# A 512-column product ahead of each score step of the row maxima, and doubled replications in the first six rounds of the scans

## The chip, the cores and the metric

The kernel runs on one core of one Trainium2 chip. The metric is the device time of one execution in microseconds (us). "PE" is TensorE (its weight loads are the separate engine name PEld), "DVE" is VectorE, "ACT" is ScalarE, "POOL" is GpSimd and "SP" is SyncE, which issues the transfers. The clock of PE that the profile calls granted has two levels here, 2.4 GHz (shown as 1.0) and 1.2 GHz (shown as 0.5); a value in between is the mean over a stretch that saw both.

## The reference

Eight images of 64 channels and 32 x 32 = 1024 tokens go through three layers:

```python
x = _mamba(...)            # W_in, causal conv, selective scan over 1024 tokens, gate, W_out
x = silu(group_norm(x)) + x_hsi
t = t + attention(layernorm(t))      # 8 heads of 8 channels, causal over 1024 tokens
t = t + moe(layernorm(t))            # 8 experts of 64 x 64, top 2 of 8 by a softmax router
```

The selective scan has 128 channels with 16 states each, h = exp(dt A) h + dt B x, y = C h.

## The kernel before

A program on every engine runs `pipeline`: twelve iterations, in each of which up to five images are in work at different stages: `a` (load), `c` (convolution, dt, B and C, then the scans), `p` (output of the scan layer, group norm, layer norm, queries and keys), `b` (attention) and `f` (projection and experts). Image `b` appears from the fourth iteration to the eleventh; `c` from the second to the ninth. So eight iterations hold attention work, and in the last two of these there is no `c`. Below, such an iteration goes by the number of the image in its attention, 1 to 8; the clock of "image 5" is that of the fifth iteration with attention.

Each iteration has two phases.

**Row maxima (score phase).** Before the softmax the kernel needs the maximum of each row of scores. 48 score steps (`SCORE_STEPS`, line 334) go over row blocks i = 0 to 7 of 128 queries, in two quads of four heads. Step s computes on PE the scores of one block of 128 queries: for i below 4 two heads with 128(i+1) keys each, for i from 4 on one head with 512 + 128(i-3) keys; a product with a mask (128 columns, line 1202) is added on the diagonal. It writes the bank pair 4, 5 or 6, 7 by turns (line 1194), and DVE then takes the maxima of the pair with one TENSOR_REDUCE (`row_maxima`, line 926). PE waits before step s until DVE is done with step s-2 (line 1192). Between the steps both engines carry the work of images `c` and `p`, at places written out by hand in the two tables `beside`: on PE, convolution at steps 1 and 2, the last folds at 1 to 3, gate projection at 5 and 6, output projection at 9 and 10, the product for dt at 11 and 12, the B product at 17 and 18, the C product at 20 and 21, the value projection at 24, transposes at 26, 33 and 34, the query and key projection at 37 and 38. These are float32 products, of which one of 512 columns is two instructions. PE executes all in program order, so a score step stands behind the work that was put before it.

**Scans and attention (round phase).** 28 rounds (`UNITS_IN`, line 336). A round holds up to two units of the scans for image `c`: `unit` (line 1253) replicates a half (512 columns) of the rows of dt and then of u over 128 partitions with a bf16 product each (`replicate`, line 1236), into the next bank of a ring of five (`free_bank`, which waits until the reader of five users earlier is done). ACT makes `decay` from the dt bank (line 762), DVE makes `drive` from the u bank (line 979), and DVE runs one scan (line 970) per two units; POOL multiplies by C (line 660); PE folds (line 1126). From the fifth round on a round also holds a step of the attention for image `b` (`weigh`, line 1302, exponentials on ACT at line 801, `add_values`, line 1317), and turns of image `f` (lines 1111, 1117, 1286). The first six rounds are four without an attention step, where `s` is `None`, and the steps s = 0 and 1; they hold 2, 2, 2, 1, 0 and 2 units.

The score phase ends with four small DVE operations on the maxima (lines 944 to 951) and eight transposes (`turn_maxima`, line 1229); SP takes the maxima out and into `q_stack` (lines 561 and 564) before the first attention step. SP issues all transfers in one order: the rows of dt and u in three parts (line 539), then the token-major copy, the parts of queries and keys, the maxima.

Of the kernel before, what the change touches and what calls it, by code (L numbers as in the profile page):

```python
# [12 lines left out]
BANK = 512  # L13
# [30 lines left out]
def mamba_attention_moe(nc, x, W_in, conv_w, conv_b, W_x, W_dt, b_dt, A_log, D, W_out, gn_gamma, gn_beta,  # L44
# [8 lines left out]
    DH = C // H  # L53
# [24 lines left out]
    with ExitStack() as ctx:  # L78
        def sb(name, shape, dt=F32):
            return ctx.enter_context(nc.sbuf_tensor(name, shape, dt))  # L80

        ps = ctx.enter_context(nc.psum_tensor("ps", [P, 8, BANK], F32))

        def banks(n, k=1):
            return ps[:, n:n + k, :].rearrange("p a b -> p (a b)")
# [39 lines left out]
        dt_rows = sb("dt_rows", [96, NG, T], BF16)  # L125
        u_rows = sb("u_rows", [96, NG, T], BF16)
# [11 lines left out]
        dt, u = read[:, 0, :], read[:, 1, :]  # L138
# [19 lines left out]
        q_stack = sb("q_stack", [P, H, T], BF16)  # L158
        k_stack = sb("k_stack", [P, H, T], BF16)
# [157 lines left out]
        def signal(name, per, base=0):  # L317
            return Signal(ctx, nc, name, per, base)
# [48 lines left out]
        dt_rep = signal("dt_rep", UNITS)  # L367
        u_rep = signal("u_rep", UNITS)
# [83 lines left out]
        def chunk(k):  # L452

            g, q = k % NG, k // NG
            return g, q, JG * g + q

        def halves(n):
            return slice(n * BANK, (n + 1) * BANK)

        def tokens(i):  # L460
            return slice(i * P, (i + 1) * P)
# [37 lines left out]
        def bank_read(user, c, b, f):  # L499

            kind, n = user
            return {"dt": (decayed, c), "u": (driven, c), "scores": (exped, b), "heads": (attn_ready, b),
                    "attn_t": (attn_t_copied, f), "proj": (t2_ready, f), "xn_t": (xnt_copied[1], f),
                    "router": (gate_centred, f), "expert": (weighted, f), "out_t": (x_out_copied, f)}[kind] + (n + 1,)
# [7 lines left out]
        with nc.Block() as block:  # L512
# [588 lines left out]
            def _(pe):  # L1101
                def program(_, c, p, b, f):

                    def project(weights, src, bank, h, rows=P):

                        return pe.matmul(ps[0:rows, bank + h, :], weights, src[:, halves(h)], start=True, stop=True)  # L1106

                    def to_channels(src, blocks, dst):

                        for n, i in enumerate(blocks):  # L1110
                            last = pe.transpose(dst[0:C, tokens(n)], src[:, i, :], ident[:, :])  # L1111
                        return last
# [75 lines left out]
                    def score_step(s):  # L1188

                        i, h0, nh = SCORE_STEPS[s]  # L1190
                        if s >= 2:
                            pe.wait_ge(row_maxed.sem, row_maxed.at(b, s - 1))
                        for hh in range(nh):
                            for h in range(i // QB + 1):
                                bank = 4 + 2 * (s % 2) + hh + h
                                diagonal = h == i // QB
                                w = P * (i % QB + 1) if diagonal else BANK
                                last = pe.matmul(ps[:, bank, 0:w], q_stack[0:9 * DH, h0 + hh, tokens(i)],  # L1198
                                                 k_stack[0:9 * DH, h0 + hh, h * BANK:h * BANK + w],
                                                 start=True, stop=not diagonal)  # L1200
                                if diagonal:
                                    last = pe.matmul(ps[:, bank, w - P:w], ident_bf[:, :], mask_q[:, :],  # L1202
                                                     start=False, stop=True)
                        last.then_inc(scores_ps.sem, 1)
# [21 lines left out]
                    def turn_maxima():  # L1226
                        pe.wait_ge(max_parts_ready.sem, max_parts_ready.at(b, 1))
                        for i in range(TB):
                            last = pe.transpose(banks(ACC).bitcast(BF16)[0:3 * H, tokens(i)],
                                                max_parts[:, i, :, :].rearrange("p r h -> p (r h)"), ident_bf[:, :])  # L1230
                        last.then_inc(max_t_ps.sem, 1)

                    def replicate(k2, bank, rows):

                        g, q, _ = chunk(k2 // 2)
                        return pe.matmul(bank, pick[:, q, :, :].rearrange("p n e -> p (n e)"),  # L1236
                                         rows[:, g, halves(k2 % 2)], start=True, stop=True)
# [4 lines left out]
                    def free_bank(user):  # L1242

                        place = places[user]
                        bank = RING[place % len(RING)]
                        if place >= len(RING):
                            read_by, batch, count = bank_read(users[place - len(RING)], c, b, f)
                            pe.wait_ge(read_by.sem, read_by.at(batch, count))
                        elif b and bank > ACC:
                            pe.wait_ge(row_maxed.sem, row_maxed.at(b, NSCORE))  # L1250
                        return banks(bank)

                    def unit(k2):
                        if k2 == 0:
                            pe.wait_ge(dt_rows_in.sem, dt_rows_in.at(c, 16 * 3 * NG))
                            pe.wait_ge(c_copied.sem, c_copied.at(c, 1))
                        replicate(k2, free_bank(("dt", k2)), dt_rows).then_inc(dt_rep.sem, 1)
                        if k2 == 0:
                            pe.wait_ge(u_rows_in.sem, u_rows_in.at(c, 16 * 3 * NG))
                        replicate(k2, free_bank(("u", k2)), u_rows).then_inc(u_rep.sem, 1)  # L1260

                    def take_turn(turn):

# [30 lines left out]
                    def weigh(s, heads):  # L1294

                        n, quad, half, j = KEY_STEPS[s]
                        lo = max(half * BANK, j * P)
                        w = (half + 1) * BANK - lo
                        diagonal = lo == j * P
                        for hq in heads:  # L1300
                            head, bank = quad * QUAD + hq, free_bank(("scores", QUAD * s + hq))
                            last = pe.matmul(bank[:, 0:w], k_stack[0:KQ, head, tokens(j)],  # L1302
                                             q_stack[0:KQ, head, lo:lo + w], start=True, stop=not diagonal)
                            if diagonal:
                                last = pe.matmul(bank[:, 0:P], ident_bf[:, :], mask_k[:, :],  # L1305
                                                 start=False, stop=True)
                            last.then_inc(weights_ps.sem, 1)
# [25 lines left out]
                    for n, (s, units, turns) in enumerate(ROUNDS):  # L1333
                        at_step = b and s is not None
                        if at_step:
                            if s == 0:
                                pe.wait_ge(max_in.sem, max_in.at(b, 16))
                            weigh(s, range(QUAD - 1))
                        if c and units:
                            unit(units[0])  # L1340
                        if b and n == 0:
                            turn_maxima()
                        if at_step:
                            if s > 0:
                                add_values(s - 1)
                            weigh(s, (QUAD - 1,))
                            if s - LAG in LAST_STEP:
                                heads_to_tokens(LAST_STEP.index(s - LAG))
                        if c:
                            for q, h, at in FOLDS:  # L1350
                                if at == n:
                                    if q == 0 and h == 0 and p:
                                        pe.wait_ge(qk_rest.sem, qk_rest.at(p, 1))
                                    fold_round(c, q, h)
                            for k2 in units[1:]:
                                unit(k2)
                        if f:
                            for turn in turns:
                                take_turn(turn)
# [8 lines left out]
                    for read_by, (batch, count) in last_read.items():  # L1368
                        pe.wait_ge(read_by.sem, read_by.at(batch, count))
                pipeline(pe, program)  # L1370


# [20 lines left out]
```

## Time and profile before

| | us |
|---|---|
| median of 3 runs | 1633.64 |
| lowest and highest | 1631.91, 1634.67 |
| the profiled execution, whole | 1626.1 |
| its span, first to last instruction | 1624.0 |
| mean granted clock of PE over the span | 0.761 |
| busy: PE, DVE, ACT, POOL | 1260.7, 1171.9, 704.3, 512.2 |

The profiled execution is 7.5 us below the median of the runs. PE's busy time counts a pipelined matmul from its start to its modelled end, so two matmuls in a row overlap; the distance between their starts is what one costs.

### The profile page before, as it was taken

The numbers are of one execution on the slowest core, as the hardware profiler recorded it, in microseconds if no ns is written. First come the engines' busy times: TensorE is split into PE (matmuls) and PEld (weight loads), VectorE is DVE, ScalarE is ACT, GpSimd is POOL, SyncE is SP. The second block draws the span as 40 slices with busy tenths as digits, with TensorE's granted clock in tenths as the row PEclk, the third lists the DMA queues.
The fourth block names the chain that finished last, engine by engine and source line by source line (L and its number), as shares of the span: only waits on it lengthen the run. The fifth ranks groups of instructions, "written<-read, shape, count | busy, mean of one in ns | idle before, by whom it ended". The sixth has DMA issues, their size and how long they took to land. (4 is left out here: it accounts for less than half of the span.)

```text
span 1624.0 us, 17597 instructions
## 1 busy us (share of the span) xinstructions
PE 1260.7 (78%) x6388; PEld 499.9 (31%) x6388; DVE 1171.9 (72%) x1388; ACT 704.3 (43%) x1298; POOL 512.2 (32%) x272
## 2 busy tenths in 40 slices
PE   2455346888888987888887987888888988899894
PEld 1111111323233333333333323333233324433433
DVE  3396398787678968887679867887688867348345
ACT  1423322347434762376335642476326631460470
POOL 2454454344334332342243333342144321000000
PEclk9567556659966998589867997599758985695696
DMA  1100320021202111201211120201220120020000
GB/s 38 45 1 13 83 53 13 7 68 30 55 8 68 30 32 38 67 1 30 62 29 45 30 50 19 68 10 23 47 61 14 30 49 17 19 51 21 3 14 7
DMA packets 25863, 54.87 MB, mean 34 GB/s; under 512 B 8531, under 2 KB 8919, under 8 KB 23448
## 3 DMA queue, kind: packets, MB, share of 16 engines
q1 hardware_dynamic: 25776, 53.73, 14.6%
q8 instruction: 51, 0.84, 0.2%
q14 instruction: 36, 0.29, 0.1%
HBM read 28.15 MB, written 12.98 MB: 25 GB/s over the span
## 5 line engine op out<-in xcount | busy, mean ns | idle before, releaser
L926 DVE TENSOR_REDUCE row_max<-ps 128x1 f32<-128x768 f32 (+7 forms) x384 | 355.9, 952 | 142.2 <-PE ps L1202 139.6
L660 POOL TENSOR_TENSOR read<-state,c_rep 128x1024 f32<-128x1024 f32 x128 | 303.9, 2374 | 466.2 <-DVE state L970 450.6
L801 ACT ACTIVATE probs<-ps 128x512 f32<-128x512 f32 (+3 forms) x768 | 329.5, 496 | 144.7 <-PE ps L1305 86.5
L970 DVE TENSOR_TENSOR_SCAN state<-decay,drive 128x1024 f32<-128x1024 f32 x128 | 357.1, 2790 | 1.8 <-POOL read L660 1.1
L1198 PE MATMUL ps<-k_stack,q_stack 72*128 72x512 bf16 (+3 forms) x768 | 280.6, 456 | 83.2 <-DVE row_max L926 64.3
L1302 PE MATMUL ps<-q_stack,k_stack 75*128 75x512 bf16 (+3 forms) x768 | 222.8, 353 | 32.7 <-DVE drive L979 17.8
L979 DVE TENSOR_TENSOR drive<-ps,b_rep 128x512 f32<-128x512 f32 x256 | 169.6, 676 | 105.7 <-PE ps L1236 105.0
L762 ACT ACTIVATE decay<-ps,a_scale 128x512 f32<-128x512 f32 x256 | 175.3, 696 | 116.8 <-DVE state L970 100.1
L1236 PE MATMUL ps<-dt_rows,pick 96*128 96x512 bf16 x256 | 120.5, 471 | 96.9 <-DVE drive L979 69.5
L1317 PE MATMUL ps<-probs,v_aug 128*32 128x512 f32 (+3 forms) x1536 | 177.4, 536 | 4.1 <-ACT acc_sb L790 1.6
L1198 PEld LDWEIGHTS ps<-k_stack,q_stack 72*128 72x128 bf16 x768 | 73.8, 116 | 274.2 <-DVE row_max L926 171.4
L1302 PEld LDWEIGHTS ps<-q_stack,k_stack 75*128 75x128 bf16 x768 | 76.2, 102 | 245.4 <-ACT probs L801 89.4
L1202 PE MATMUL ps<-mask_q,ident_bf 128*128 128x128 bf16 x512 | 137.7, 278 | 0.0
L1236 PE MATMUL ps<-u_rows,pick 96*128 96x512 bf16 x256 | 120.8, 472 | 19.9 <-DVE attn L996 5.5
L1305 PE MATMUL ps<-mask_k,ident_bf 128*128 128x128 bf16 x512 | 110.4, 235 | 0.0
L597 POOL TENSOR_TENSOR ln_s<-ln_s,minus_half 128x8 f32<-128x8 f32 x16 | 26.3, 1643 | 262.2 <-DVE ln_s L904 262.2
L1202 PEld LDWEIGHTS ps<-mask_q,ident_bf 128*128 128x128 bf16 x512 | 65.2, 127 | 62.2 <-issue 54.2
L1236 PEld LDWEIGHTS ps<-dt_rows,pick 96*128 96x128 bf16 x256 | 27.4, 107 | 161.3 <-DVE drive L979 104.2
L1061 DVE TENSOR_TENSOR moe<-ps,gate_e 128x512 f32<-128x512 f32 x64 | 43.8, 685 | 44.9 <-PE ps L1286 44.9
L1126 PE MATMUL ps<-read,fold 128*32 128x512 f32 x512 | 74.6, 683 | 0.8 <-POOL read L660 0.8
L1106 PE MATMUL ps<-xc,w_bc 128*128 128x512 f32 x64 | 57.8, 1015 | 22.4 <-ACT b_rep L719 18.2
L1286 PE MATMUL ps<-w_expert,xn_t 96*128 96x512 f32 x128 | 69.3, 653 | 0.8 <-ACT decay L762 0.8
(169 smaller groups left out, 1281.6 us busy)
## 6 DMA issues: line engine op xcount, KB each, us to landing
q_stack<-q_parts_dram SPq DMA_DIRECT2D x48, 192.0 KB
k_stack<-k_parts_dram SPq DMA_DIRECT2D x48, 192.0 KB
dt_rows<-read SPq DMA_DIRECT2D x96, 64.0 KB, 2.0
u_rows<-read SPq DMA_DIRECT2D x96, 64.0 KB, 2.0
k_parts_dram<-read SPq DMA_DIRECT2D x40, 128.0 KB, 2.4
q_parts_dram<-read SPq DMA_DIRECT2D x24, 128.0 KB, 2.3
xs<-in_x SPq DMA_DIRECT2D x8, 256.0 KB, 3.5
residual<-in_x SPq DMA_DIRECT2D x8, 256.0 KB, 9.6
```

Of the source, the lines that this page charges most:

```text
L660: pool.tensor_tensor(read[:, k % (2 * NG), :], state[:, k % 2, :], c_rep[:, :], ALU.mult)\
L762: act.activation(decay[:, k % 2, halves(h)], bank_of(("dt", k2)), ACT.Exp, scale=a_scale[:, j:j + 1])\
L801: act.activation(probs[:, e % (2 * QUAD), 0:w], bank_of(("scores", e))[:, 0:w], ACT.Exp, scale=SCALE).then_inc(exped.sem, 1)
L926: dve.tensor_reduce(row_max[:, i, h0:h0 + nh], scores[:, :, 0:P * (i + 1)], AX.X, ALU.max, negate=True).then_inc(row_maxed.sem, 1)
L970: dve.tensor_tensor_scan(state[:, k % 2, :], decay[:, k % 2, :], drive[:, k % 3, :], 0.0, ALU.mult, ALU.add).then_inc(scanned.sem, 1)
L979: dve.tensor_tensor(drive[:, k % 3, halves(h)], bank_of(("u", k2)), b_rep[:, halves(h)], ALU.mult)\
L1198: last = pe.matmul(ps[:, bank, 0:w], q_stack[0:9 * DH, h0 + hh, tokens(i)], k_stack[0:9 * DH, h0 + hh, h * BANK:h * BANK + w], start=True, ...
L1202: last = pe.matmul(ps[:, bank, w - P:w], ident_bf[:, :], mask_q[:, :], start=False, stop=True)
L1236: return pe.matmul(bank, pick[:, q, :, :].rearrange("p n e -> p (n e)"), rows[:, g, halves(k2 % 2)], start=True, stop=True)
L1302: last = pe.matmul(bank[:, 0:w], k_stack[0:KQ, head, tokens(j)], q_stack[0:KQ, head, lo:lo + w], start=True, stop=not diagonal)
L1305: last = pe.matmul(bank[:, 0:P], ident_bf[:, :], mask_k[:, :], start=False, stop=True)
L1317: last = pe.matmul(ps[GW * hq:GW * (hq + 1), ACC, lo:BANK], v_aug[:, j, quad * QUAD + hq, :], probs[:, (QUAD * s + hq) % (2 * QUAD), 0:BAN ...
```

## The change

Each of the 48 score steps of an image first issues one more product of 72 rows, 128 weight columns and 512 moving columns, from the same stacks, into the first bank of the pair that the step is about to write. The step's own first product overwrites it. In the first six rounds of a round phase each unit issues the replication of dt twice and that of u twice into the same bank; only the second signals the reader. The waits are the same and stand where they stood.

```diff
+                    def keep_clock(bank, weights, src):
+
+                        pe.matmul(bank, weights, src, start=True, stop=True)
+
...
                         i, h0, nh = SCORE_STEPS[s]
                         if s >= 2:
                             pe.wait_ge(row_maxed.sem, row_maxed.at(b, s - 1))
+                        keep_clock(ps[:, 4 + 2 * (s % 2), :], q_stack[0:9 * DH, h0, tokens(i)],
+                                   k_stack[0:9 * DH, h0, 0:BANK])
...
-                    def unit(k2):
+                    def unit(k2, again=False):
                         if k2 == 0:
                             pe.wait_ge(dt_rows_in.sem, dt_rows_in.at(c, 16 * 3 * NG))
                             pe.wait_ge(c_copied.sem, c_copied.at(c, 1))
-                        replicate(k2, free_bank(("dt", k2)), dt_rows).then_inc(dt_rep.sem, 1)
+                        bank = free_bank(("dt", k2))
+                        if again:
+                            replicate(k2, bank, dt_rows)
+                        replicate(k2, bank, dt_rows).then_inc(dt_rep.sem, 1)
                         if k2 == 0:
                             pe.wait_ge(u_rows_in.sem, u_rows_in.at(c, 16 * 3 * NG))
-                        replicate(k2, free_bank(("u", k2)), u_rows).then_inc(u_rep.sem, 1)
+                        bank = free_bank(("u", k2))
+                        if again:
+                            replicate(k2, bank, u_rows)
+                        replicate(k2, bank, u_rows).then_inc(u_rep.sem, 1)
...
                         if c and units:
-                            unit(units[0])
+                            unit(units[0], s is None or s < 2)
...
                             for k2 in units[1:]:
-                                unit(k2)
+                                unit(k2, s is None or s < 2)
```

## Rows read from the trace of the kernel before

**Rows 1.** The page: busy time of DVE, granted PE clock in 40 slices, maxima group.

```profile
PE 1260.7 (78%) x6388; PEld 499.9 (31%) x6388; DVE 1171.9 (72%) x1388; ACT 704.3 (43%) x1298; POOL 512.2 (32%) x272
PEclk9567556659966998589867997599758985695696
L926 DVE TENSOR_REDUCE row_max<-ps 128x1 f32<-128x768 f32 (+7 forms) x384 | 355.9, 952 | 142.2 <-PE ps L1202 139.6
```

**Rows 2.** Busy time by stretch, score phases of images 2, 4, 5, 7 and 8.

```profile
core 0: us, PE busy (x) PEld busy (x) DVE busy (x) ACT busy (x) POOL busy (x), PEclk, DMA share, GB/s
428.40:502.10 73.70, 60.15 (x253) 24.56 (x252) 55.63 (x69) 21.50 (x22) 24.20 (x13) 0.73 0.21 47
...
780.80:858.40 77.60, 65.39 (x252) 25.88 (x251) 56.11 (x69) 21.54 (x22) 24.18 (x13) 0.67 0.23 53
960.30:1035.60 75.30, 62.30 (x252) 24.69 (x251) 55.87 (x70) 21.60 (x22) 24.21 (x13) 0.70 0.23 56
...
1318.70:1388.40 69.70, 58.32 (x230) 23.40 (x225) 52.78 (x68) 6.46 (x7) 11.09 (x7) 0.57 0.19 41
1459.60:1511.00 51.40, 45.35 (x172) 18.05 (x169) 44.78 (x49) 0.00 (x0) 0.00 (x0) 0.53 0.10 24
```

**Rows 3.** Busy time by stretch, columns as in rows 2: round phases, image 5 and 7.

```profile
1035.60:1045.10 9.50, 7.86 (x37) 4.56 (x38) 7.91 (x12) 5.76 (x9) 2.24 (x1) 0.64 0.37 85
1045.10:1056.00 10.90, 7.73 (x33) 2.68 (x32) 9.57 (x11) 4.87 (x10) 4.26 (x4) 0.53 0.01 2
1056.00:1139.20 83.20, 73.04 (x483) 27.89 (x480) 67.87 (x80) 55.58 (x122) 32.14 (x14) 0.96 0.10 21
1388.40:1407.50 19.10, 15.98 (x78) 9.04 (x78) 5.30 (x12) 6.59 (x16) 1.64 (x1) 0.50 0.02 6
```

**Rows 4.** Timeline of PE: 512-column products in a row, from 1034.08 and from 1056.52.

```profile
1034.08 0.63 PE L1236 MATMUL ps<-dt_rows,pick 96*128 96x512 bf16 x1
1034.51 0.63 PE L1236 MATMUL ps<-u_rows,pick 96*128 96x512 bf16 x1
...
1056.52 0.38 PE L1236 MATMUL ps<-dt_rows,pick 96*128 96x512 bf16 x1
1056.74 0.38 PE L1236 MATMUL ps<-u_rows,pick 96*128 96x512 bf16 x1
```

**Rows 5.** Timeline of DVE, steps 37 and 38: image 5, then image 2.

```profile
1020.54 0.96 DVE L926 TENSOR_REDUCE row_max<-ps 128x1 f32<-128x768 f32 x1 [1.60 <-PE ps L1202]
1023.10 1.82 DVE L926 TENSOR_REDUCE row_max<-ps 128x1 f32<-128x768 f32 x2 [1.60 <-PE ps L1202]
...
488.76 0.96 DVE L926 TENSOR_REDUCE row_max<-ps 128x1 f32<-128x768 f32 x1 [0.34 <-PE ps L1202]
490.06 2.82 DVE L926 TENSOR_REDUCE row_max<-ps 128x1 f32<-128x768 f32 x3 [0.34 <-PE ps L1202]
```

**Rows 6.** Line 926, waits for PE (us, times), image 4, window 795 to 804 us.

```profile
  PE ps L1202: 3.9, 3
```

**Rows 7.** Line 926, waits for PE (us, times), image 5, windows 976:984, 986:1003, 1003.5:1017.5, 1017.5:1035.7.

```profile
  PE ps L1202: 0.4, 1
...
  PE ps L1202: 6.3, 5
...
  PE ps L1202: 1.8, 5
...
  PE ps L1202: 3.8, 4
```

**Rows 8.** Timeline of ACT, image 5, after the last operation of the group norm on DVE.

```profile
988.69 1.20 ACT L683 ACTIVATE read<-ps,gn_v 64x1024 f32<-64x1024 f32 x1 [4.72 <-DVE gn_v L874]
...
993.26 0.99 ACT L719 COPY b_rep<-ps 128x1024 f32<-128x1024 f32 x1
```

**Rows 9.** Line 926, waits for PE (us, times), image 8, window 1459 to 1511 us.

```profile
  PE ps L1202: 6.2, 12
```

**Rows 10.** Timeline, image 8: maxima of 1024 columns, PE's two products and mask for one.

```profile
1478.80 4.82 DVE L926 TENSOR_REDUCE row_max<-ps 128x1 f32<-128x1024 f32 x4 [0.23 <-PE ps L1202]
1480.08 1.03 PE L1198 MATMUL ps<-k_stack,q_stack 72*128 72x512 bf16 x2 [0.31 <-DVE row_max L926]
```

**Rows 11.** Who waited for whom on DVE, image 5, window 1036 to 1058 us.

```profile
DVE drive L979 <- PE ps L1236: 3.8, 3, 1.7
```

## Prediction

> **What bounds the kernel now.** No engine is full: DVE works 72% of the span and PE's 78% counts overlapping matmuls whole, and PE's clock moves between its levels all the time [rows 1]. I read first the groups of instructions, for who is waited for: before the 384 maxima DVE stands idle 142.2 us, 139.6 of them for PE [rows 1]. Then the stretches by phase: a score phase takes 73.7 to 77.6 us for six images, 69.7 and 51.4 for the last two, with DVE busy 56, 52.8 and 44.8, at a mean clock of 0.73 down to 0.53 [rows 2]. The round phase runs at 0.96 once it is past its first 20 us, which are at 0.64 and 0.53 in image 5, and at 0.50 where there are no scans [rows 3]. So the low clock sits where the change adds products, and DVE waits for PE in just these stretches. In the score phase DVE is the path, with PE on it wherever a score step stands behind other work.
>
> Is the low clock what makes DVE wait? The same two steps tell it. At steps 37 and 38, behind the query and key projection, DVE idles 1.60 us each in image 5, and 0.34 each in image 2, where the clock was high for a few microseconds [rows 5]. At steps 9 to 11 image 4 loses 3.9 us at the low clock and image 5 loses 0.4 at the high one [rows 6, 7].
>
> **What is added, and its price.** 384 products in the score phases (48 x 8). In the rounds 9 units x 2 products x 8 images = 144. From start to start a 512-column product takes 0.43 us at the low clock and 0.22 at the high one [rows 4]. That is 528 products and 116 us of PE at the high clock, 227 at the low. What counts is whether PE with it is later than DVE. A steady pair of steps shows the margin. PE begins step s when DVE is done with s-2, and has the length of one reduction. At 1024 columns, low clock, the own work is 512 + 512 + 128 columns, 0.96 us at 0.43 per 512, and DVE still idles 0.23 per two steps; four reductions take 4.82 us [rows 10]. A pair there lasts 1.23 + 1.23; so handing over costs 1.23 - 0.96 = 0.27. At the high clock with the product the step has 1664 columns, 0.70 us, and 0.97 with the handing over: below the 1.14 of a reduction back to back, so hidden. At 640 columns it is 0.54 + 0.27 = 0.81 against about 0.74, a little exposed, less than now (0.64 + 0.27 = 0.91). So at the high clock a step with the product costs PE less time than the bare step at the low one for every block from i = 1 on (1280 columns against 768, 0.54 against 0.64 us), and the same at i = 0.
>
> **The sum, if the clock stays high through most of the score phase:**
> - Steps 36 to 47: 3.8 us idle now [rows 7]; 0.34 + 0.34 as in image 2 [rows 5] and 0.22 for each of two added products, 1.1. Saved 2.7 in six images (1 and 3 to 7), and +0.4 in image 2: -15.8.
> - Steps 9 to 11: 3.9 to 0.4 + 0.4, 3.1 saved in the four images that are low there (1, 4, 6, 7); +0.4 in the three that are high: -11.2.
> - Steps 16 to 21: 6.3 us idle [rows 7]. Not all is PE's. Behind the group norm ACT works without a pause from 988.69 to 994.25 (988.69 to 993.26 and 0.99 more) before the C product can start [rows 8]; that chain of 5.6 us stays. I take 1.3 saved in six images, for the B and C products at the high clock: -7.8.
> - Steps 24 to 35: 1.8 [rows 7] to 0.6, and somewhat more in image 7: -8.4 over seven images.
> - Image 8: 6.2 idle [rows 9] to about 3 (the value projection halves; blocks of 640 and 256 columns stay a little exposed): -3.
> - Steps 0 to 2, where the clock is high already and DVE waits for POOL, fold and score in a row: three products of 0.22 on the path in seven images: +4.6.
>
> Together -41.6. Waits of chains will still pull the clock down here and there; I take 85% of it: -35. Bounds: -50 (all of it and the steady pairs too) and, with the clock never up, the slower rival below.
> - First rounds with scans, images 1 to 6: DVE idles 3.8 us for replications [rows 11], at low clock. A doubled replication at the high clock costs what the single one costs now (2 x 0.22 against 0.43), so the units gain nothing; what gains is the other PE work there (transposes, weigh, values). At the high clock I get about 2 us an image back; if the clock falls in round 3 or 4, where PE has little, the two units of round 5 cost 4 x 0.43 = 1.7 more. I take -1 each, -6, with bounds -15 and +12.
> - The two iterations with scans but no attention: DVE is never late for PE there once running; only the first unit is exposed, up to 0.9 us each: +2.
> - First rounds of images 7 and 8, 19 us at 0.50 each [rows 3]: no product is added; if the phase is entered at the high clock, -2 each: -4.
>
> Sum -43: the profiled 1626.1 to 1583, and the median 1633.6 to about **1590**. (The profiled execution lies 7.5 below the median; I apply the same difference to both.)
>
> **What is late next.** Behind the score phase stand the rows of u. PE takes u's first replication at 1034.51 without waiting [rows 4], so the slack of the transfers isn't visible as a wait; if the tail of the score phase shrinks by 5 us and the chain from the layer norm through ACT, POOL and SP only by 3, the rest is lost before the first drive.
>
> A rule that speaks against the change: by the Trainium skill, "TensorE: Matmul & The Clock Gate", section "Part 3: Packing small matmuls — row/col tiling", a weight load overlaps running matmuls only when it goes to other row groups. The added product brings a load of 128 columns on the same rows. Rows 4 have a load for each product and 0.43 and 0.22 us from start to start, as long as the same product's columns at two clocks in the ratio of two, so I count no load. By the rule the result would be the fifth rival's.
>
> **The rivals.**
> 1. The clock rises for about half of the score phase only. Then half of the savings come (-20) and in the low half PE sets the pace with 0.43 per step wherever it is within 0.1 us of DVE: 192 steps, half of them, some 0.1 to 0.2 each, +14; first rounds +3. About 1631 to 1610, say 1620. For it: the clock falls now wherever chains of small operations stop PE (steps 13 to 17), and those stay. Chance 0.15.
> 2. The rows of u, or SP's issue order, become late, 2 to 3 us an image in six images: 1590 + 15 = 1605. Chance 0.10. It would show as DVE or PE waiting for a transfer at the head of the rounds.
> 3. Slower: the clock stays low in the score phases. In image 8 PE is already busy 45.4 of 51.4 us and yet at 0.53 [rows 2], so a busy PE alone doesn't raise it. Then each step is PE's: with 1664 columns 1.40 us against 1.23 now, with 1280 1.08 against 0.87, small ones +0.25; on average 0.19 x 384 = 73 us, and the first rounds 6 x 3 = 18: about 1725. It decides from the point where the added columns don't lift the clock. Against it: the added product makes up half again of the array's work in a step (512 on an average of 939 columns), and a PE that never waits is what stands ahead of the rises seen. A milder form (high in the middle, low around) ends at 1640 to 1660. Chance 0.09, both.
> 4. The doubled replications cost more than the score phases bring in beside them: low clock in round 5 and exposed doubling, +3 an image for six: 1590 + 24 = 1614. Chance 0.03.
> 5. The weight load isn't hidden: 0.10 us (24.7 us of 251 loads, [rows 2]) on each of the steps where PE is close, about half of 384, +19: 1609. The forecast's mechanism with a smaller gain; chance 0.03.
>
> **How the numbers follow.** Forecast 0.60, its own range 1572 to 1608. A measurement of this kernel can tell some 0.2%, 3.3 us. Faster by more: forecast 0.60, nearly all of rivals 1, 2, 4 and 5 and the forecast's neighbours, 0.85 together. Slower: rival 3 and a little of 1, 0.10. The same: 0.05. The range reaches down to all of the sum with the first rounds at their good bound (1633.6 - 50 - 15) and up into rival 1: 1568 to 1620.
>
> **What would show it.** Right: granted clock over 0.85 in the score phases of images 1 to 7; steps 37 and 38 idle about 0.55 each in every image; idle before line 926 from 142 us down to some 100; image 8's score phase near 48 us, image 4's near 68. The first rounds: mean clock over 0.75 and idle before line 979 below 3 us. Wrong: score phases at 0.6 with PE never waiting for DVE (rival 3), waits for transfers at line 1236 (rival 2), or a steady pair at 1024 columns that takes longer than 2.46 us.

## The result, and the profile after

| | before | after |
|---|---|---|
| median of 3 runs, us | 1633.64 | 1683.32 |
| lowest and highest | 1631.91, 1634.67 | 1674.09, 1683.7 |
| ratio, 95% interval | | 1.029 [1.025, 1.034] |
| profiled execution, its span | 1626.1, 1624.0 | 1674.1, 1672.0 |
| mean granted clock over the span | 0.761 | 0.809 |

The change makes the kernel 3% slower; 1590 was forecast. The clock did rise, and the time rose with it.

The same stretches as in [rows 2] and [rows 3], in the profile after (score phases of images 2, 4, 5, 7 and 8 and the sum over all eight, then image 5's round phase in three parts and the first rounds of image 7):

```profile
core 0: us, PE busy (x) PEld busy (x) DVE busy (x) ACT busy (x) POOL busy (x), PEclk, DMA share, GB/s
...
438.70:520.40 81.70, 72.44 (x301) 30.12 (x300) 56.17 (x69) 21.12 (x22) 23.88 (x13) 0.75 0.23 53
...
810.20:886.90 76.70, 67.04 (x301) 28.73 (x300) 56.05 (x69) 21.08 (x22) 24.02 (x13) 0.81 0.23 53
992.60:1070.40 77.80, 68.28 (x301) 28.99 (x300) 56.16 (x69) 21.14 (x22) 24.02 (x13) 0.80 0.23 56
...
1359.20:1429.30 70.10, 62.73 (x277) 28.00 (x270) 53.20 (x67) 6.46 (x7) 10.84 (x7) 0.70 0.19 40
1500.70:1561.00 60.30, 56.99 (x219) 25.09 (x217) 46.01 (x50) 0.00 (x0) 0.00 (x0) 0.58 0.09 20
sum 605.20, PE 536.58 PEld 230.06 DVE 435.99 ACT 133.06 POOL 156.25; mean PE 67.07 PEld 28.76 DVE 54.50 ACT 16.63 POOL 19.53
...
1070.40:1080.00 9.60, 8.33 (x37) 3.84 (x36) 6.71 (x12) 5.44 (x8) 0.94 (x1) 0.69 0.28 67
1080.00:1091.50 11.50, 8.10 (x41) 4.13 (x39) 10.19 (x11) 5.41 (x11) 4.86 (x3) 0.79 0.00 1
1091.50:1175.10 83.60, 73.77 (x491) 27.99 (x491) 68.20 (x81) 55.78 (x123) 33.05 (x15) 0.97 0.10 22
1429.30:1448.00 18.70, 15.51 (x74) 8.60 (x75) 5.34 (x13) 6.22 (x14) 1.64 (x1) 0.50 0.03 6
```

The sum of the score phases goes from 575.5 (the same eight stretches before) to 605.2 us: +29.7. The round phases go from 782.1 to 796.0, +13.9, and the first score phase starts at 270.8 instead of 266.4, +4.4. Together these are the 48.0 us between the spans. The mean clock of the score phases rises only from 0.66 to 0.75. Image 8 is the plainest: no other work stands between its steps but the value projection, PE is now busy 57 of 60 us, and the clock is 0.58. Before, that phase took 51.4. The 0.58 is the mean of two stretches: 9.2 us of a high clock that was there when the phase began, and the low one from then to the end, though PE is busy 49.55 of these 51.1 us.

```profile
1500.70:1509.90 9.20, 7.43 (x49) 3.59 (x48) 8.20 (x11) 0.00 (x0) 0.00 (x0) 1.00 0.57 130
1509.90:1561.00 51.10, 49.55 (x172) 21.50 (x170) 37.80 (x40) 0.00 (x0) 0.00 (x0) 0.50 0.00 0
```

Its last steps, by the timeline of DVE and of PE:

```profile
1555.47 1.22 DVE L926 TENSOR_REDUCE row_max<-ps 128x1 f32<-128x1024 f32 x1 [0.38 <-PE ps L1208]
1556.85 1.22 DVE L926 TENSOR_REDUCE row_max<-ps 128x1 f32<-128x1024 f32 x1 [0.16 <-PE ps L1208]
1558.35 1.22 DVE L926 TENSOR_REDUCE row_max<-ps 128x1 f32<-128x1024 f32 x1 [0.28 <-PE ps L1208]
1559.74 1.23 DVE L926 TENSOR_REDUCE row_max<-ps 128x1 f32<-128x1024 f32 x1 [0.16 <-PE ps L1208]
```

```profile
1555.22 0.63 PE L1110 MATMUL ps<-k_stack,q_stack 72*128 72x512 bf16 x1
1555.65 1.06 PE L1204 MATMUL ps<-k_stack,q_stack 72*128 72x512 bf16 x2
1556.50 0.31 PE L1208 MATMUL ps<-mask_q,ident_bf 128*128 128x128 bf16 x1
1556.75 0.61 PE L1110 MATMUL ps<-k_stack,q_stack 72*128 72x512 bf16 x1
```

The added product (line 1110) takes 0.43 us of the array (1555.22 to 1555.65), and none of these reductions begins without a wait: (1559.74 - 1555.47) / 3 = 1.42 us a step, where it was 1.23. PE issues product after product and the clock stays at 1.2 GHz.

Where the clock is high amid the other work, the steps behave as forecast. Steps 37 and 38 of image 4 (high clock) and of image 5 (low), answering to [rows 5]:

```profile
871.88 0.96 DVE L926 TENSOR_REDUCE row_max<-ps 128x1 f32<-128x768 f32 x1 [0.56 <-PE ps L1208]
873.40 2.97 DVE L926 TENSOR_REDUCE row_max<-ps 128x1 f32<-128x768 f32 x3 [0.56 <-PE ps L1208]
...
1053.23 0.96 DVE L926 TENSOR_REDUCE row_max<-ps 128x1 f32<-128x768 f32 x1 [2.03 <-PE ps L1208]
1056.21 0.96 DVE L926 TENSOR_REDUCE row_max<-ps 128x1 f32<-128x768 f32 x1 [2.03 <-PE ps L1208]
```

0.56 where 0.34 + 0.22 was worked out, and 2.03 = 1.60 + 0.43 where the clock is low.

The first drives of image 5's round phase, answering to [rows 11]; line 1242 is the replication:

```profile
1074.30 0.69 DVE L979 TENSOR_TENSOR drive<-ps,b_rep 128x512 f32<-128x512 f32 x1 [2.34 <-PE ps L1242]
...
1076.01 0.69 DVE L979 TENSOR_TENSOR drive<-ps,b_rep 128x512 f32<-128x512 f32 x1 [0.43 <-PE ps L1242]
...
1091.78 0.69 DVE L979 TENSOR_TENSOR drive<-ps,b_rep 128x512 f32<-128x512 f32 x1 [1.45 <-PE ps L1242]
```

Together with the drive after them they wait 6.6 us, where 3.8 were waited before: 2.34 was 1.49, 0.43 was nothing, 1.45 was 0.60. Each is later by one or two products at the low clock.

### The profile page after: what moved, and what is told of

Same layout as the page of the kernel before. It is cut to its first block and busy times, and to the rows that moved or that the text cites. A ratio compares the mean times of both kernels' runs of the same rounds, so it can differ in the third digit from the quotient of the medians.

```text
span 1672.0 us, 18653 instructions
## 1 busy us (share of the span) xinstructions
PE 1337.7 (80%) x6916; PEld 546.8 (33%) x6916; DVE 1173.2 (70%) x1388; ACT 704.5 (42%) x1298; POOL 511.8 (31%) x272
## 5 line engine op out<-in xcount | busy, mean ns | idle before, releaser
L1204 PE MATMUL ps<-k_stack,q_stack 72*128 72x512 bf16 (+3 forms) x768 | 262.8, 421 | 0.0
L1314 PE MATMUL ps<-q_stack,k_stack 75*128 75x512 bf16 (+3 forms) x768 | 219.0, 347 | 35.5 <-DVE drive L979 18.0
L1110 PE MATMUL ps<-k_stack,q_stack 72*128 72x512 bf16 x384 | 188.8, 492 | 61.2 <-DVE row_max L926 45.7
L1242 PE MATMUL ps<-dt_rows,pick 96*128 96x512 bf16 x328 | 138.1, 461 | 92.4 <-DVE drive L979 65.5
L1242 PE MATMUL ps<-u_rows,pick 96*128 96x512 bf16 x328 | 136.9, 457 | 19.7 <-DVE attn L996 6.9
L1208 PE MATMUL ps<-mask_q,ident_bf 128*128 128x128 bf16 x512 | 127.9, 258 | 0.0
L1204 PEld LDWEIGHTS ps<-k_stack,q_stack 72*128 72x128 bf16 x768 | 90.7, 118 | 87.2 <-issue 67.5
L1110 PEld LDWEIGHTS ps<-k_stack,q_stack 72*128 72x128 bf16 x384 | 42.6, 111 | 175.8 <-DVE row_max L926 119.1
L1208 PEld LDWEIGHTS ps<-mask_q,ident_bf 128*128 128x128 bf16 x512 | 61.0, 119 | 72.7 <-issue 47.6
L1242 PEld LDWEIGHTS ps<-dt_rows,pick 96*128 96x128 bf16 x328 | 33.2, 109 | 157.6 <-DVE drive L979 96.0
```

Source lines behind the costliest of these rows:

```text
L1110: pe.matmul(bank, weights, src, start=True, stop=True)
```

## The experiments

The theory after the result: PE's clock is not lifted in this kernel by products that use 72 of the array's 128 rows, though they keep PE busy; at the low clock the added product is then a plain cost. The rivals: that the doubled replications make the loss; that the other operands or the data matter and not the rows; that only the time PE is occupied counts. All runs have the kernel before beside them on the same chip. All times are medians in us, with the ratio to the kernel before and its interval.

**The two parts alone.** The argument `s is None or s < 2` taken out of the calls of `unit`, so that nothing is doubled (e1), and the call of `keep_clock` taken out (e2).

> The added 72-row product in the score steps alone, the replications as before. My theory after the result: the product costs 0.43 us wherever PE sets the pace, because the clock is not raised by products of 72 rows, although PE then never waits. It expects most of the loss here: the eight score phases some 30 us longer together (605 against 575 us in the two profiles), the round phases as before, so 1655 to 1670 us, and image 8's score phase near 60 us at a clock of about 0.58. The rival, that the doubled replications make the loss, expects 1630 to 1645.

1666.5, ratio 1.022 [1.017, 1.027]. Score phases 617.6 us in its profile, image 8's 63.5:

```profile
1496.80:1560.30 63.50, 61.79 (x219) 27.16 (x217) 46.35 (x49) 0.00 (x0) 0.00 (x0) 0.50 0.08 18
```

PE is busy 61.8 of 63.5 us and the clock is at 1.2 GHz throughout. The added score product by itself makes two thirds of the loss (34.7 of 51.7 us over the kernel before, with f1 below for the whole change).

> The doubled replications of the first six rounds alone. My theory: 10 to 18 us of the loss, from the round phases (796 against 782 us in the two profiles) and the start, so 1643 to 1652 us, idle before the drive (line 979) up by some 20 us. The rival, that the doubling is harmless and the loss is all in the score phase, expects 1631 to 1637.

1631.9 against 1631.8, ratio 1.001 [0.998, 1.004]. The time followed the rival, though the waits followed the theory: the page's group of the drive has

```profile
L979 DVE TENSOR_TENSOR drive<-ps,b_rep 128x512 f32<-128x512 f32 x256 | 169.9, 678 | 127.0 <-PE ps L1240 126.5
```

where the kernel before waits 105.7 us. This is taken up again below.

**The rows of the added product.** The doubling stays out; the product in the score step becomes

```diff
-keep_clock(ps[:, 4 + 2 * (s % 2), :], q_stack[0:9 * DH, h0, tokens(i)],
-           k_stack[0:9 * DH, h0, 0:BANK])
+keep_clock(ps[:, 4 + 2 * (s % 2), :], ident_bf[:, :],
+           mask_q[:, :].unsqueeze(1).to_broadcast([P, BANK // P, P]))
```

> As e1, but the added product has 128 rows (the identity as weights, the mask repeated four times as the moving operand), 512 columns as before. If the clock follows how many rows of the array the products use, it rises in the score phases: image 8's score phase at 0.85 or more and 47 to 50 us long, the time below that of e1 by 25 us or more and perhaps below 1625. If only the time that PE is occupied counts, or if the data count (these are mostly zeros), the result is that of e1, within 5 us, with image 8's score phase at 0.58 and 60 us.

1610.7, ratio 0.989 [0.985, 0.993]: 56 us below the same product with 72 rows. Score phases of images 3 and 8, and the sum of the eight:

```profile
609.00:679.80 70.80, 57.92 (x299) 25.54 (x298) 55.51 (x69) 21.84 (x22) 24.04 (x13) 0.95 0.23 54
...
1451.30:1498.10 46.80, 37.90 (x219) 17.16 (x217) 44.05 (x49) 0.00 (x0) 0.00 (x0) 1.00 0.12 27
sum 561.10, PE 463.83 PEld 201.82 DVE 431.45 ACT 136.15 POOL 156.28; mean PE 57.98 PEld 25.23 DVE 53.93 ACT 17.02 POOL 19.53
```

Image 8 runs at 2.4 GHz from its first step to its last. Its instructions are those of e1 but for the added product of each step (48 of the 219), which has 56 more rows and other operands. In this phase the forecast's step from the clock to the time holds: 46.8 us, where about 48 was forecast. Over all eight phases it doesn't; that is taken up under the reasons. On DVE, the reductions of 896 and 1024 columns stand back to back, the added product hidden as worked out:

```profile
1489.42 8.70 DVE L926 TENSOR_REDUCE row_max<-ps 128x1 f32<-128x896 f32 x8
```

The operands were changed too, so a control has the same identity and mask, cut to 72 rows (`ident_bf[0:9 * DH, :]` and `mask_q[0:9 * DH, :]`).

> The control for the 128-row product: the same operands (identity and repeated mask), cut to 72 rows, 512 columns, no doubling. If it is the rows that raise the clock, this is as slow as the product from the stacks, 1655 to 1675 us, image 8's score phase at a clock below 0.7 and over 57 us. If it was the other operands (other weights than the next product's, mostly zeros), it is as fast as with 128 rows, 1605 to 1620.

1664.6, ratio 1.023 [1.019, 1.027], image 8:

```profile
1493.40:1553.50 60.10, 56.87 (x219) 25.00 (x217) 45.99 (x49) 0.00 (x0) 0.00 (x0) 0.58 0.09 21
```

As slow as e1 with its other operands, and 54 us slower than e3, from which only the rows differ. Operands and data are out; the rows are left. Between the two, 96 rows:

> The added product of identity and repeated mask with 96 rows, between the 72 (1665 us) and the 128 (1611 us). 72 rows reach into the third group of 32 rows, 96 fill it. If the whole groups of 32 that a product touches count, it is as slow as 72 rows, 1655 to 1670; if the rows count one by one, it lies between, 1625 to 1650, with image 8's score phase partly at the high clock.

1632.9, ratio 1.001 [0.997, 1.005]. It lies between (1665, 1633, 1611), which speaks against whole groups of 32: 72 and 96 rows touch the same three. Images 6 and 8:

```profile
1145.00:1217.60 72.60, 60.97 (x299) 26.54 (x298) 55.84 (x69) 21.50 (x22) 24.00 (x13) 0.89 0.23 52
1462.50:1522.90 60.40, 57.17 (x219) 25.13 (x217) 45.95 (x49) 0.00 (x0) 0.00 (x0) 0.57 0.09 20
```

Where float32 products of the other images stand between the steps, 96 rows bring the phase to 0.89 (image 6 is at 0.78 in the profile of the change); where the steps stand alone they don't lift it, and image 8 is as slow as with 72. I had expected image 8 to be partly high; only its first 8.9 us are, as with 72 rows.

And 128 rows with fewer columns, `ps[:, bank, 0:288]` from `mask_q[:, 0:96]` repeated three times:

> The added product with 128 rows but only 288 columns, so that rows times columns are those of 72 rows and 512 columns. If the clock follows rows times columns, it falls short of the 512-column form: some of the score phases at the low clock, but the product is also shorter by 0.09 us at the high clock; 1600 to 1640 us. If 128 rows are enough whatever the columns, the clock is as high as with 512 columns and the time lower than 1611 by 10 us or more.

1612.9, ratio 0.989 [0.985, 0.993]. The runs spread widely, seven of them from 1601.9 to 1620.7 and one at 1629.2 (the median without it is 1611.6). Images 6 and 8:

```profile
1124.40:1196.30 71.90, 57.95 (x299) 26.74 (x298) 55.86 (x69) 21.57 (x22) 23.83 (x13) 0.88 0.21 49
1438.40:1491.40 53.00, 46.17 (x219) 22.77 (x217) 44.88 (x50) 0.00 (x0) 0.00 (x0) 0.69 0.10 24
```

Both happen at once: the clock falls short of the 512-column form (0.69 against 1.00 in image 8), and the shorter product costs less where it is high. So rows alone don't do it either; rows and columns both count. No run here fixes how.

Split at the change of level, the image 8 phases say more than their means. With 72 rows (f3), 96 rows (f4) and 128 rows of 288 columns (f5) the clock is 1.00 for the first 9.4, 8.9 and 19.8 us and 0.50 for the 50.7, 51.5 and 33.2 us that are left; it doesn't come back in the phase. With 128 rows it does: f2 below has 0.86 in the first 8.2 us of that phase and 0.99 in the 39.2 after, and e4 has 1.00, then 0.78 for 7.7 us, then 1.00 for the last 28.4.

**No added product at all: the step's own products over 128 rows.** PE spends the same time on a product of 72 rows and of 128: at the high clock a 512-column one takes 0.22 us from its start to the next in both (871.08 to 871.30 in the profile after, 1490.57 to 1490.79 in e3). So the rows can be filled without a column more, if the further ones hold zeros:

```diff
-last = pe.matmul(ps[:, bank, 0:w], q_stack[0:9 * DH, h0 + hh, tokens(i)],
-                 k_stack[0:9 * DH, h0 + hh, h * BANK:h * BANK + w],
+last = pe.matmul(ps[:, bank, 0:w], q_stack[:, h0 + hh, tokens(i)],
+                 k_stack[:, h0 + hh, h * BANK:h * BANK + w],
...
+dve.memset(q_stack[64:P, :, :], 0.0)      # once, in the setup
+dve.memset(k_stack[96:P, :, :], 0.0)
...
+sp.dma_start(q_stack[KQ - 3:KQ, heads, :], k_stack[96:99, heads, :])   # per image and quad
```

The transfer clears rows 72 to 74, which hold the maxima of the image before.

> No added product. The score step's own products run over all 128 rows instead of 72; the further rows are zero in the queries' stack (rows 72 to 74 are filled with zeros by one more transfer per half of the heads, the rest once at the start). PE's columns are those of the kernel before. If the number of rows counts whatever they hold, the clock rises in part of the score phases, since the own products are now up to 1.8 times the work: mean clock there from 0.66 to 0.80 or more, and 1600 to 1620 us. If it doesn't, 1630 to 1640 us.

1572.6, ratio 0.965 [0.961, 0.968]: well below what I expected. Score phases of images 2, 3, 7 and 8:

```profile
429.10:500.60 71.50, 55.06 (x248) 22.86 (x251) 55.31 (x70) 21.59 (x22) 24.32 (x13) 0.81 0.24 50
602.50:668.60 66.10, 47.00 (x247) 20.32 (x250) 54.88 (x69) 22.08 (x22) 24.21 (x13) 0.94 0.26 58
1285.00:1343.60 58.60, 41.47 (x226) 17.35 (x227) 52.13 (x67) 6.46 (x7) 11.13 (x7) 0.85 0.23 50
1414.10:1458.40 44.30, 28.52 (x168) 12.54 (x169) 42.97 (x49) 0.00 (x0) 0.00 (x0) 0.96 0.15 32
```

The page's group of the maxima (line 930 here) shows that the idle time before them has gone from 142.2 to 91.4 us:

```profile
L930 DVE TENSOR_REDUCE row_max<-ps 128x1 f32<-128x768 f32 (+7 forms) x384 | 348.6, 950 | 91.4 <-PE ps L1206 89.5
```

In image 8 PE is busy 28.5 us instead of the 45.4 of [rows 2], for the same products (four of the 172 records are missing; g1 below, with 171 of them, has 29.2), and the clock is high: a PE that is busy for less time, over more rows, is granted more. So rows count here though the weights are zero in all 56 of them; the other operand holds ones in 24 and zeros in 32.

The first score phase begins at 275.4 there, 9 us later than before. The zeros moved from the setup to the start of the main program on DVE, with a semaphore for SP:

> The score step's own products over 128 rows as in the run that gave 1573, but the zeros are written on DVE at the start of the main program, where DVE waits for the first images, and not in the setup ahead of it. The first score phase began at 275.4 there against 266.4 in the kernel before; if the zeros made that, this is 5 to 9 us less, 1564 to 1568; otherwise 1572.

1566.1, ratio 0.960 [0.958, 0.963], first score phase at 268.8: as expected. Beside it, the softmax weights' products (75 rows) and the replications (96) over 128 rows too, with zeros in `pick`, `dt_rows` and `u_rows` from row 96:

> As the run beside it, and also the products for the softmax weights (75 rows) and the replications (96 rows) go over 128 rows, the further ones zero. If more rows lift the clock in the first rounds as they did in the score phases, the first 20 us of the round phases rise above 0.6 and the idle before the drive falls by 10 us or more: 1545 to 1560. If the first rounds are low for want of work rather than rows, no difference, within 5 us.

1564.9, ratio 0.958 [0.956, 0.961]. No difference that can be told: the medians are 1.2 us apart and the intervals overlap. The first rounds of image 5 stay where they were, here g2 and then g1, the run without these rows:

```profile
1008.60:1018.10 9.50, 8.14 (x38) 4.53 (x37) 7.89 (x12) 5.79 (x9) 2.21 (x1) 0.64 0.53 123
1018.10:1029.00 10.90, 7.70 (x34) 2.69 (x32) 9.60 (x11) 4.87 (x10) 4.26 (x4) 0.54 0.01 2
```

```profile
1008.80:1018.30 9.50, 8.11 (x38) 4.50 (x37) 7.88 (x13) 5.28 (x8) 2.17 (x1) 0.64 0.53 124
1018.30:1029.20 10.90, 7.05 (x34) 2.61 (x33) 9.64 (x11) 4.87 (x10) 4.26 (x4) 0.57 0.01 2
```

In the second stretch DVE is busy 9.6 of 10.9 us, and PE waits 2.5 us for ACT's `decay` and 0.7 for DVE's `drive`. The round phases as a whole are 9 us shorter in g2's profile (771 against 780), 4 of them in the last one, while its start and score phases are 4.5 longer; with one execution of each, a small gain from these rows is neither shown nor excluded.

**The doubled replications.** First the change as it is, and the change with the 128-row product.

> The change as it is, once more, on the chip of the three runs beside it. Score product alone gave 1666 us and doubling alone no difference, while the change gave 1683; if the parts add up, this is 1660 to 1672 us here and the 1683 was another chip or another phase of the clock; if the doubling costs only beside the score product, it is 1675 to 1690.

1683.6, ratio 1.034 [1.028, 1.039]: the first measurement stands, 17 us over e1.

> The change with the added score product over 128 rows (identity and mask) in place of 72, the doubled replications kept. By the rows theory 1605 to 1625 us, about as the 128-row product without doubling (1611); the theory by which the doubling costs beside a score product expects 1625 or more.

1627.7, ratio 0.998 [0.996, 1.001]: again 17 us over the run without doubling (1610.7), and outside what I gave the rows theory. So doubling costs 17 us beside either product. Does it cost without an added product? On the fastest form:

> The doubled replications on top of the fastest form so far (own products over 128 rows, zeros written late, 1566 us). If the doubling costs some 2.5 us in each iteration with scans whenever the clock is low there, as the waits before the drive show (+14 to +21 us in every profile with it), this is 1578 to 1586 us. If it costs only beside an added score product, 1563 to 1570.

1583.4, ratio 0.972 [0.969, 0.975]: 17 us again over 1566.1, which was measured on another chip; against the kernel before, the ratio goes from 0.960 to 0.972. So it costs without an added product too. And alone once more:

> The doubled replications alone, once more and in five rounds: 1632 us before, +2 with an interval of -3 to +7, though the waits before the drive grew by 21 us in its profile. If the cost is really offset when it stands alone, because the busier first rounds leave PE at the high clock elsewhere, the ratio is again within 0.3% of one; if the first result was a matter of phase, it is 1.005 to 1.01.

1631.1 against 1629.1, ratio 1.002 [1.000, 1.004]. So the 17 us are missing when the doubling stands alone, twice. Sums of the score phases in the profiles of e2 and h2:

```profile
sum 570.10, PE 480.62 PEld 194.13 DVE 433.82 ACT 133.44 POOL 157.57; mean PE 60.08 PEld 24.27 DVE 54.23 ACT 16.68 POOL 19.70
```

```profile
sum 564.00, PE 470.51 PEld 192.73 DVE 432.81 ACT 133.17 POOL 157.50; mean PE 58.81 PEld 24.09 DVE 54.10 ACT 16.65 POOL 19.69
```

575.5 before. The round phases are 15 and 13 us longer (797 and 795 against 782) and the start 6 and 3.5, and the score phases are 5 and 11 us shorter although nothing in them is changed. With the added 128-row product they don't shrink by the doubling (561.1 and 561.6 us for e3 and f2). That points to the score phases as the place of the offset, but it doesn't show it: each is a single execution, the clock of the score phases is 0.66 before, 0.67 in e2 and 0.68 in h2, and the kernel before itself takes from 1614.8 to 1635.5 us in the 17 executions beside h2. Why the doubling costs 17 us on three forms and nothing that can be told on the kernel before stays open.

## Why the prediction was wrong

**The step that failed** is the condition in front of the sum, "if the clock stays high through most of the score phase". I counted the added product in columns ("half again of the array's work in a step") and never in rows, though every row of the trace names them: 72 of 128. In image 8, PE that never waits is at 0.50 to 0.58 with 72 rows and at 1.00 with 128. [Rows 2] already had the warning, PE busy 45.4 of 51.4 us at 0.53. I used it for rival 3, and then let it weigh 0.09.

**Rival 3** was the outcome, between its two forms: a score phase where each step at the low clock is PE's. Its price was right (1.40 us forecast for a 1024-column step, 1.42 measured) and its total too large (about 1725 against 1683), because the clock is still high in part of each phase, 0.75 in the mean; its milder form (1640 to 1660) was too small. In the profile of the change the high parts lie around the float32 products of the other images (image 5: 1.00 in steps 0 to 11, 0.50 in steps 36 to 47); that these products lift the clock is read from this, and no run tests it. Where the clock was high the price came as forecast: steps 37 and 38 wait 0.56 us each in image 4, and 2.03 in image 5, where it was low.

**A second step failed: the sum itself.** f2 is the kernel of the forecast with its condition met. Its score phases are at 0.86 to 0.95 in images 1 to 6, 0.77 in image 7 and 0.97 in image 8, and yet it takes 1627.7 us and not 1590; its score phases are 13.9 us shorter than before, where 35 were forecast. The pages of e3 and e4 show the idle time before the maxima, 142.2 before:

```profile
L926 DVE TENSOR_REDUCE row_max<-ps 128x1 f32<-128x768 f32 (+7 forms) x384 | 354.1, 952 | 131.3 <-PE ps L1208 128.8
```

The forecast had about 100, and e4, without an added product, has 91.4. By the terms of the sum, from the timelines of DVE (waits for PE of 0.15 us and more, summed; images 1 to 7, and image 8 by itself):

| | forecast change | before | e3 | e4 |
|---|---|---|---|---|
| steps 0 to 2 | +4.6 | 38.9 | 43.5 | 38.6 |
| steps 9 to 11 | -11.2 | 16.5 | 9.2 | 3.0 |
| steps 16 to 21 | -7.8 | 38.9 | 41.7 | 33.6 |
| steps 24 to 35 | -8.4 | 15.9 | 17.6 | 7.1 |
| steps 36 to 47 | -15.8 | 23.2 | 13.6 | 5.7 |
| image 8 | -3 | 6.2 | 3.2 | 1.4 |
| together | -41.6 | 139.6 | 128.8 | 89.5 |

The prices for the high clock were about right: where e3 has it through the whole stretch, steps 36 to 47 idle 1.1 us (image 3; 1.1 forecast) and steps 9 to 11 mostly 1.0 (0.8 forecast). What was wrong is "I take 85% of it": the clock still dips, and in a dip the added product is paid on top of the low clock. In steps 16 to 21 image 5 of e3 is at 0.89 and idles 5.1 us, 1.2 less than before (1.3 forecast); image 6 is at 0.77 and idles 7.8, 1.5 more than before. One wait of each, image 5 and image 6:

```profile
996.30 1.23 DVE L926 TENSOR_REDUCE row_max<-ps 128x1 f32<-128x1024 f32 x1 [2.55 <-PE ps L1208]
...
1171.31 1.23 DVE L926 TENSOR_REDUCE row_max<-ps 128x1 f32<-128x1024 f32 x1 [5.50 <-PE ps L1208]
```

e3 and e4 have nearly the same mean clock in the score phases (0.89 and 0.87), and e3 idles 39 us more, about as much as its time is longer (1610.7 against 1572.6). My estimate from this pair: the lifted clock gives back some 50 us of this idle time in either, and the 384 added products take 39 of them, 0.10 us each. The clock, not the added work, was what there was to gain.

**Term by term.** Score phases: -35 forecast, +29.7 measured (+40 in the profile of f1, the same kernel again, 616.0). First rounds of images 1 to 6 and the two iterations without attention: -6 and +2 forecast; the round phases of images 1 to 6 show +15, the start +4.4. That is beyond the bound of +12 for the first. The mistake in it was to expect the high clock there: the first round comes after the tail of the score phase, which is low, so a doubled unit takes 1.7 us and not 0.9, at the first round (+0.85 and +0.43 in image 5) and at the sixth (+0.85 and +0.6). First rounds of images 7 and 8: -4 forecast; image 7's are still at 0.50 and 18.7 us long, where they were 19.1, and image 8's round phase is 2 us shorter. [Rows 4] are no evidence on the weight loads, since they list none; the page does (as many PEld as PE, 6388).

**What held:** the low clock is what makes DVE wait in the score phase. e3 and e4 took 21 and 59 us from the kernel by lifting it. The hidden reductions of 896 and 1024 columns held too. The transfers of u (rival 2) did not come up: DVE's waits for the drive are all for PE, and PE's own waits for the rows of dt and u, 48.4 and 10.2 us before, are 49.7 and 7.9. The doubled replications cost 17 us with the clock high in the score phases (f2 against e3); the forecast had -4 for the first rounds and the scans without attention, and rival 4, at a chance of 0.03, +18 for them. The weight load of the added product costs nothing on the path: line 1204 starts 0.43 us after line 1110 on the same rows. So the rule of the Trainium skill cited for rival 5 doesn't describe this trace.

By the Trainium skill, "TensorE: Matmul & The Clock Gate", section "Part 1: The HAM clock gate (the "warmup" mystery)", the clock is granted by how busy PE has been. Image 8 after the change is busy 57 of 60 us and at 0.58; in e4 it is busy 28.5 of 44.3 us and at 0.96. The measurement decides: in this kernel the time that PE is occupied doesn't settle the clock by itself; the rows of its products count as well.

## What to carry to other kernels

If PE is at the low clock though it hardly waits, look at the partitions of its products before adding any. Widening products that are there to 128 rows with zeros costs no column and gave 4.0% here; an added product of 72 rows cost 2.2%, and of 128 rows gained 1.2%. An added product on the path of a step is paid at the clock that is there, so price it at the low one until a run shows the high one, and price the stretches where the clock dips by themselves: a mean of 0.89 over a phase hid them here. Doubling instructions in a stretch that waits for another engine brings nothing while that engine is the bound.

## What the hardware showed that I had not expected

- The same 384 added products of 512 columns, by rows: 72 rows 1664.6 us, 96 rows 1632.9, 128 rows 1610.7, beside 1632.0, 1631.5 and 1631.8 for the kernel before. In the stretch where they stand alone (image 8) the mean clock is 0.58, 0.57 and 1.00.
- A high clock doesn't outlast a busy PE of 72-row products: in image 8 it is 1.00 for 9.2 us and then 0.50 for 51.1, with PE busy 49.55 of them.
- Rows in which the weights are all zero count for the clock: e4's image 8 is at 0.96 with 56 such rows of 128, against 0.53 without them.
- A mean clock over the span that rises (0.761 to 0.809) beside a time that rises by 3%. The granted clock is no measure of speed; what PE issues at it must be counted too.
- The doubled replications cost 17 us on three forms of the kernel and, alone, nothing that can be told (ratios 1.001 and 1.002); no run explains it.
